# A decoder layer on one core: all engines' calls in a new order, with fewer cleared-tile matmuls

## What is computed

```python
x = x + attn(layernorm(x))            # down-projection, two window branches, feed-forward
x = x + xattn(ctx, layernorm(x))      # causal softmax over 1024 context rows
x = x + ffn(layernorm(x))             # shared expert + 8 routed experts, top 2

def attn(x):
    xi = rmsnorm(x @ down_w + down_b)
    o1 = branch(xi[:, :32], window=10, shift=5)      # 8 heads of 4 channels
    o2 = branch(xi[:, 32:], window=20, shift=10)
    x = x + concat(o1, o2) @ up_w + up_b
    return x + gelu(rmsnorm(x) @ ffn_w1 + ffn_b1) @ ffn_w2 + ffn_b2

def ffn(flat):                                        # 9 experts, 128 -> 256 -> 128
    probs = softmax(flat @ router_w + router_b)
    w = keep_top2(probs)
    h1 = gelu(einsum('td,edh->teh', flat, rw1) + rb1)
    mixed = einsum('ted,te->td', einsum('teh,ehd->ted', h1, rw2) + rb2, w)
    return gelu(flat @ sw1 + sb1) @ sw2 + sb2 + mixed
```

## Time and profile before

| what | value |
|---|---|
| time, three runs | 167.3, 171.09 (median) and 172.68 us |
| profiled execution, its time | 167.33 us |
| profiled execution, its span | 165.5 us |
| PE busy | 150.9 us (91%) |
| VectorE busy | 131.4 us (79%) |
| ScalarE busy | 102.7 us (62%) |
| POOL busy | 42.6 us (26%) |
| mean granted TensorE clock | 0.983 of full speed |
| DMA moved | 13.12 MB |

### The profile page before, as it was taken

How to read it: one execution, slowest core, us unless ns; L and a number is a source line. 1 busy time by engine, 2 the same in 40 slices (tenths; PEclk the granted TensorE clock), 3 DMA queues, 4 the chain that set the end, 5 groups by cost and what they waited for, 6 DMA issues and landing times.

```text
span 165.5 us, 3243 instructions
## 1 busy us (share of the span) xinstructions
PE 150.9 (91%) x1188; PEld 113.4 (68%) x1188; DVE 131.4 (79%) x236; ACT 102.7 (62%) x176; POOL 42.6 (26%) x59
## 2 busy tenths in 40 slices
PE   0798999999989987989899999999999999999980
PEld 0646875659966567788565858768887878887840
DVE  3797898999972999986555659999879866999960
ACT  3113371526173486566787797987987798996830
POOL 5359999202000404005430030033160000000000
PEclk9999999999999999999978999999999999999997
DMA  5999100600870000000096089000000009802002
GB/s 143 365 303 407 61 0 0 117 20 0 143 143 4 0 0 2 0 4 0 0 157 128 8 242 267 5 0 0 0 2 0 4 4 235 272 0 65 0 0 67
DMA packets 6176, 13.12 MB, mean 79 GB/s; under 512 B 672, under 2 KB 2333, under 8 KB 5904
## 3 DMA queue, kind: packets, MB, share of 16 engines
q1 hardware_dynamic: 4902, 9.70, 18.8%
q0 software_dynamic: 944, 2.88, 9.7%
q10 hardware_dynamic: 314, 0.32, 0.7%
HBM read 11.81 MB, written 0.56 MB: 75 GB/s over the span
## 4 chain that ended last, share of the span: by engine, by line
PE 75%; DVE 10%; issue 4%; DMA 2%; POOL 2%; ACT 2%; POOLq 1%; DVEq 0%; ACTq 0%
PE ps L1478 63%; PE ps L1481 5%; PE ps L1754 3%; DMA x_sb<-in_x 2%; PE ps L1548 1%; POOL rstd L582 1%; DVE st L1064 1%; POOL rstd L580 1%; POOLq L94 1%; DVE room L1313 1%; PE ps L1678 1%; DVE room L1058 1%; DVE xf_lo L1261 1%; PE ps L1794 1%; PE ps L1638 1%
## 5 line engine op out<-in xcount | busy, mean ns | idle before, releaser
L1326 DVE TENSOR_TENSOR low<-room,high 128x1024 fp32r<-128x1024 f32 (+1 forms) x20 | 22.1, 1112 | 4.0 <-ACT high L894 3.7
L878 ACT ACTIVATE room<-ps,consts_sb 128x512 f32<-128x512 f32 x36 | 23.2, 682 | 1.5 <-PE ps L1478 0.9
L894 ACT ACTIVATE high<-room 128x1024 fp32r<-128x1024 f32 (+1 forms) x20 | 19.1, 970 | 4.2 <-DVE room L1313 3.5
L580 POOL TENSOR_SCALAR rstd<-mv 128x1 f32<-128x1 f32 (+4 forms) x13 | 5.5, 425 | 54.6 <-DVE mv L1245 32.3
L1478 PE MATMUL ps<-xf_hi,w_hi 128*128 128x512 f32 x36 | 16.7, 463 | 0.0
L1313 DVE TENSOR_TENSOR room<-room,gates 128x1024 f32<-128x1024 f32 (+1 forms) x13 | 14.7, 1136 | 1.0 <-ACT room L878 0.7
L1478 PE MATMUL ps<-xf_lo,w_hi 128*128 128x512 f32 x36 | 14.8, 412 | 0.4 <-DVE xf_lo L1261 0.4
L582 POOL TENSOR_TENSOR rstd<-rstd,minus_half 128x1 f32<-128x1 f32 (+4 forms) x18 | 14.5, 804 | 1.9
L592 POOL TENSOR_SCALAR xn<-x_sb,mv,rstd 128x128 f32<-128x128 f32 x8 | 14.9, 1874 | 0.0
L1478 PE MATMUL ps<-high,w_hi 128*128 128x512 f32 x36 | 14.6, 407 | 0.0
L1478 PE MATMUL ps<-xf_hi,w_lo 128*128 128x512 f32 x36 | 14.6, 405 | 0.0
(11 more groups left out here) (204 smaller groups left out, 342.1 us busy)
## 6 DMA issues: line engine op xcount, KB each, us to landing
gates<-gate_rows SPq DMA_DIRECT2D x12, 256.0 KB, 5.4
moe_w_sb<-in_moe_w SPq DMA_DIRECT2D x2, 1152.0 KB, 11.7
w_lo<-in_moe_w POOLq DMA_DIRECT2D x2, 1152.0 KB, 9.0
ffn_hids<-gate_rows SPq DMA_DIRECT2D x4, 256.0 KB, 3.9
pr<-in_ctx SPq DMA_DIRECT2D x1, 576.0 KB, 6.6
xs<-xn POOLq DMA_DIRECT2D x1, 512.0 KB, 5.2
out<-acc SPq DMA_DIRECT2D x8, 64.0 KB, 1.6
ffn_hids<-in_bias SPq DMA_DIRECT2D x1, 434.7 KB
```

Of the source, the lines that this page charges most:

```text
L580: step(pool.tensor_scalar(dst, src, scale, eps, ALU.mult, ALU.add))
L878: act.activation(hidden_at(q), ps[:, z_bank(q), :], ACT.Gelu, bias=cols_sb[:, i:i + 1]).then_inc(moe_h_ready, 1)
L894: act.activation(split_part(high, h, e, a, z), hidden_part(h, e, a, z), ACT.Copy).then_inc(high_ready, 1)
L1326: dve.tensor_tensor(split_part(low, h, e, a, z), hidden_part(h, e, a, z), split_part(high, h, e, a, z).bitcast(F32), ALU.subtract).then_in ...
```

## The change

The four lists of calls of PE, VectorE, ScalarE and POOL are in a new order. No step is added or removed but for the cleared-tile matmuls: on PE all of them behind the first `qkv_rows` are taken out, and 19 are put in at other places, by a new helper that takes the bank and up to two semaphores. Those ahead of it (nine in all) stay as they were. SP's list is the same.

```diff
@@ PE, the new helper
+            def idle(at, after=None, count=1, also=None, to=1):
+
+                pe.wait_ge(zeros_clear, 1)
+                if after is not None:
+                    pe.wait_ge(after, count)
+                if also is not None:
+                    pe.wait_ge(also, to)
+                mm(ps[:, at, :], zeros16[:, 0:P], zeros16[:])
@@ POOL
             rstd0_pow(0)
-            clear()
             rstd0_pow(1)
             rstd1_pow(0)
             rstd1_pow(1)
+            narrow()
             xn_tiles()
             xs_add()
-            w1_low()
             rstd2_pow(0, 0)
             rstd2_pow(0, 1)
-            narrow()
             rstd3_pow(0, 0)
             rstd3_pow(0, 1)
+            w2_low()
+            w1_low()
+            clear()
             rstd4_pow(0)
             rstd4_pow(1)
             rstd4_pow(2)
             rstd4_pow(3)
-            w2_low()
             rstd2_pow(1, 0)
@@ VectorE, two of many places
             win_margins(1)
+            win_margins(0)
             x_moments(0)
-            win_margins(0)
             x_moments(1)
...
-            x3_tiles(0, 0, 4)
             moe_gate(1, 6)
...
             moe_low(1, 8, 1)
+            x3_tiles(0, 0, 4)
             x3_tiles(1, 0, 1)
```

More of the change, by code:

```diff
@@ L899, in y_copy @@
                 act.activation(x1T[h][:, a * P:z * P], ps[:, 2 + h, a * P:z * P], ACT.Copy).then_inc(y_ready, z - a)
-            half_copy()
             downc_copy()
             bias_split()
+            qkv_copy(1, 0)
+            wqc_copy()
             window_cols(0, 0)
-            qkv_copy(1, 0)
             window_cols(0, 1)
+            half_copy()
             window_cols(1, 1)
+            pu_copy()
             qkv_copy(0, 0)
             w1_high()
-            wqc_copy()
-            pu_copy()
+            w1_negate()
             window_exp(1, 0)
@@ L959, in _ @@
             ffn_gelu(1, 1, 0)
+            wT_copy(0)
             moe_high(0, 0, 0)
+            w_split(0)
+            moe_gelu(0, 1, 1)
             moe_high(0, 0, 1)
-            moe_gelu(0, 1, 1)
-            wT_copy(0)
-            w_split(0)
             moe_gelu(0, 2, 0)
+            moe_gelu(0, 2, 1)
             x1T_copy(1, 0)
-            moe_gelu(0, 2, 1)
             moe_gelu(0, 3, 0)
+            moe_gelu(0, 3, 1)
+            moe_high(0, 1)
             softmax(4)
-            moe_high(0, 1)
+            moe_high(0, 2)
             pT_copy(4)
             softmax(5)
-            moe_gelu(0, 3, 1)
             moe_gelu(0, 4, 0)
+            moe_gelu(0, 4, 1)
             pT_copy(5)
[L976 to L981, removed]
             moe_gelu(0, 5, 0)
             moe_gelu(0, 5, 1)
+            softmax(6)
+            moe_high(0, 3)
+            moe_high(0, 4)
+            pT_copy(6)
+            moe_high(0, 5)
+            softmax(7)
+            moe_gelu(0, 6, 0)
             pT_copy(7)
-            moe_high(0, 4)
-            moe_high(0, 5)
-            moe_gelu(0, 6, 0)
             moe_gelu(0, 6, 1)
-            xf_high(1, 0)
             moe_gelu(0, 7, 0)
@@ L1013, in _ @@
             moe_high(1, 2)
-            gelu_table()
+            moe_high(1, 3)
             moe_gelu(1, 4, 0)
@@ L1348, in _ @@
             xi_norm(1)
-            xs_begin()
             bias_low()
@@ L1364, in _ @@
             window_pairs(1, 1)
+            xs_begin()
             window_product(0, 1)
@@ L1982, in _ @@
             hidden(0, 3, 0)
+            hidden(0, 3, 1)
             scores(4, 0)
             scores(4, 1)
+            hidden(0, 4, 0)
+            scores(5, 0)
+            hidden(0, 4, 1)
             output(0, 0, 0)
-            scores(5, 0)
-            hidden(0, 3, 1)
+            output(0, 0, 1)
             p_columns(4, 0)
             scores(5, 1)
-            hidden(0, 4, 0)
+            output(0, 1, 0)
             p_columns(4, 1)
-            output(0, 0, 1)
+            output(0, 1, 1)
+            scores(6, 0)
             values(4)
             p_columns(5, 0)
-            scores(6, 0)
             scores(6, 1)
+            hidden(0, 5, 0)
             p_columns(5, 1)
-            hidden(0, 4, 1)
-            output(0, 1, 0)
+            hidden(0, 5, 1)
             values(5)
-            hidden(0, 5, 0)
+            output(0, 2, 0)
+            output(0, 2, 1)
             scores(7, 0)
```

246 lines of the change are left out of this document (116 added, 130 removed).

## The result

The changed kernel takes 171.94 us (median of four executions, 170.76 to 172.16) beside 169.63 us of the kernel before: a ratio of 1.024, interval 1.014 to 1.033. The time forecast, 171.5 us, is met; the sum behind it is met in part only. The profiled execution took 170.76 us with a span of 168.9, so 3.4 us more than the one before, where the sum had 2.3. Executions of one kernel differ by up to 9 us, much of it with the clock that they were granted, and every ratio here, with its interval, leaves out those far above their kernel's fastest: two of the four of the kernel before (hence 1.024, where the two medians give 1.014), four of ten of `e1_zeros_back`, four of six of `e12_swap_copy_first`.

What follows compares the result with a forecast made beforehand. PE's own work was taken to set the end from 95.6 us on, so gains lie ahead of the first expert matmul; terms summed to +2.3 us on 167.33, 169.6, plus 1.9 for spread: 171.5 us, range 166.5 to 175.5.

Steps and rivals of the forecast that it cites:

- the sum behind it: Whole kernel: 1.35 - 0.4 + 0 + 0.75 + 0.6 = +2.3 us on the profiled execution's 167.33 us, so 169.6.
- The decisive term: Two weight transfers from POOL: w1_low lands 6.6 us behind w2_low, at 84.55, and hidden(0,0,0) waits for it: +1.35 us.
- Rival B: Weight transfers: both land by 80.8 us and the wait is hidden; 164.2 to 165.9, near 167 with the spread; chance 0.20.
- the gain up to it: Ahead of the transfers: window_scores(1, 1) 2.7 us earlier, of which 1.8 us are left at the end of softmax(1).
- The walk: New order followed call by call with timeline durations: window_scores(1, 1) at 51.0 for 53.73, softmax(1) done at 66.5 for 68.34.
- the first term: Start of hidden(0,0,0), first expert matmul: 84.55 for 83.21 because it waits for w1_low, +1.35 us.
- the missing zeros: Cleared-tile matmuls on PE, 42 down to 28: PE waits instead, priced at 0 unless the clock notices.
- rival C: Window attention: clock falls as zeros are out, value_sum(1, 0) loads take 2.9 us more; 172.5, with spread 174.4; chance 0.25.
- A: The forecast itself: PE waits for w1_low ahead of the expert matmuls; 169.6 us on the profile's clock; chance 0.47.
- Front and copy: Kernel start: win_margins(0) ahead of x_moments(0) gains 0.5 us up to product(1, 0); qkv_copy(0, 0) behind pu_copy costs nothing.
- -0.4, 0 and +0.75: Behind hidden(0,0,0): PE's xf_lo wait goes, -0.4 us; low clock as before, 0; second softmax stage stalls PE, +0.75.
- Tail: Kernel end: half 0's four output issues stand right ahead of the last four in SP's queue, ending 163.3 for 162.65: +0.6 us.

Runs made afterwards that it cites:

- e1_zeros_back: Changed kernel with 12 cleared-tile matmuls put back on PE between 20 and 35 us: median 169.75 us, ratio 1.011 to the kernel before.
- e12_swap_copy_first: Changed kernel with w1_low issued first, four cleared-tile matmuls added and qkv_copy(0,0) back ahead of pu_copy: median 165.9 us, ratio 0.976 to the kernel before.
- e6_after_again: The changed kernel itself, measured again beside the kernel before on one chip: median 170.5 us, ratio 1.017.
- e3_both: Changed kernel with 12 cleared-tile matmuls put back and w1_low issued ahead of w2_low: median 170.55 us beside 169.32 us of the kernel before.
- e10_swap_again: Changed kernel with w1_low issued ahead of w2_low on POOL: median 165.03 us, ratio 0.986 to the kernel before.
- e7: Changed kernel with w1_low issued first and, from hidden(0,0,0) on, the calls in the order of the kernel before: median 166.02 us, ratio 0.989 to the kernel before.

## Why the prediction was right, and where it was not

**The decisive term held.** The two transfers follow each other: the first lands 9.1 us after its issue (9.0 used), the second 5.6 us behind the first (6.6 used). `w1_low` was issued 0.85 us behind `w2_low`, not 1.3. With `w1_low` first, the wait is gone; POOL's wait for `w2_negate`, behind which `w1_low` stood in its queue and which the prediction had in its sum, is as much part of this as the shared engines, and the runs do not separate the two.

The Trainium skill (DMA: Bandwidth & Descriptors, section Issuing engines are not separate DMA queues) says that all DMAs of a core run on the same 16 engines and interleave there. The share of 1.03 over 12.3 us agrees with the first half, for two transfers that are both issued by POOL; of interleaving these two show little, since the first lands as early as one alone.

By the fit of the Trainium skill (the same page, section Anatomy of one DMA), 2.0 us plus bytes over 436 GB/s, both would land about 7.4 us after the first issue, an estimate. The trace has 14.7 us from the first issue to the second landing, and the measurement decides.

Rival B, with both landed by 80.8 us, did not come: the landings are at 81.4 and 87.0.

**The step that failed is the gain up to it.** The walk had `window_scores(1, 1)` at 51.0, 2.7 us early, and `softmax(1)` done at 66.5; it was 55.45 and 70.0. Behind that all went nearly as said: `w2_low` issued 2.3 us after `softmax(1)` (2.45 walked), landings as above. The wait for `w1_low` therefore ended at 87.24 instead of 84.55, and the first term is +4.03 us instead of +1.35.

The difference goes with the clock: the walk took every duration from a trace at full clock, and the sum priced the missing zeros at 0. The score sums came late, so that `window_scores(1, 0)` started 1 us later (28.59 against 27.54 in `e6_after_again`, where the first dip is missing); the four matmuls of the score sides took 1.76 and 2.08 us a pair, against 1.13 and 1.12 in `e3_both`; and the value sums took 7.6 us instead of 5.34. This is what rival C spoke of, and its sign, a low clock between 13 and 70 us, came. C put its 2.9 us on the value sums alone, where the rows have 2.3 there and 2.6 ahead of them; and C came together with A, not in its place.

How much of the 2.7 us the order would give at full clock is not shown, for no run has it there without zeros in the front. With its 12 (`e3_both`) it is 0.7 us. An estimate without them: at the full-clock durations of the score sides the value sums of `e10_swap_again` would start near 37.2 instead of 38.49. Their second part waits for VectorE's last sum, done at 39.35 there, and takes 3.6 us at full clock, so it would end near 43.0, where the walk had 42.5. From there to `window_scores(1, 1)` took 8.2 us in the changed kernel and in `e3_both` alike (8.5 walked), which makes 51.2. By this the order was walked about right, and what the walk lacked was the clock, or the price of the zeros that would hold it.

Between `window_scores(1, 1)` and the end of `softmax(1)` the walk lost 0.9 us to `w2_high` and the copy; the rows show no loss there, 14.55 us against 14.61 before.

**Front and copy.** The L1075 product starts at 8.07 for 8.84: 0.77, where 0.5 was expected (8.16 to 8.47 in the ten later profiles with this front, 8.61 and 8.96 in the two with the old one). `qkv_copy(0, 0)` behind `pu_copy` was priced at nothing; `window_scores(1, 0)` comes 0.3 us late without a dip, so it cost a little.

**Behind hidden(0, 0, 0).** -0.4, 0 and +0.75 make +0.35; measured to the last addition +0.70 (78.98 against 78.28), and +0.03 in `e6_after_again` (78.31). `e7` and `e10` put the order at +0.45. The low clock behind the wait was priced at 0, because the old kernel has such a stretch too, and that was about right: it costs 0.87 us by `e6` against `e10`, and in the old order 78.28 us with it stand against 76.99 without it (`e7`), where 0.37 of the difference are the wait for `xf_lo`. Removing the wait removes this cost as well, which is why the swap gains more than the wait.

**Tail.** +0.6 was wrong. The first four output issues start at 163.01, early enough to be over before the last four: the issues end 2.1 us after the start of the last additions in both kernels. The span closed 1.3 us sooner behind them than before, which no part of the change explains: in the profiled execution of the kernel before one of the eight outputs took 2.9 us from issue to landing, in that of the changed kernel none took more than 1.6.

```profile
163.01 4.32 SPq L555 DMA_DIRECT2D out<-acc  x8
```

So 4.03 + 0.70 - 1.3 = 3.4 us on the profiled executions. A first term that was 2.7 us short met a tail that was 1.9 us too long and 1.9 us added for the spread, of which 1.2 came. That the time is hit more closely than its sum is luck.

## What to carry to other kernels

Where two large transfers are issued from one queue, the one that is read first goes first. Here the second of two landed 14.7 us after the first issue, where one alone takes 9.0; and a transfer also waits for whatever the one ahead of it in the queue waits for, here a copy that held it back by some 5 us. When an order is walked call by call with durations from a trace at full clock, say what each stretch would cost at half the clock, and give that a place in the sum and not only among the rivals. Do not count on a few cleared tiles to prevent a dip: 17 and 12 of them held the clock in some executions and not in others, four did nothing, and at full clock each costs 0.215 us of PE.

## What the hardware showed that was not expected

The granted clock differs between executions of one kernel on one chip: 0.936 to 0.990 over four executions of `e3_both`, with spans of 168.3 to 169.9 and 162.6 us, and 0.945 to 1.000 for the kernel before. The mean clock is not all of it: beside `e6_after_again` the kernel before had a span of 163.9 us at 0.986 and of 168.5 us at 0.987. One such execution says little about a change of this size. In the changed kernel the clock stayed at 1.2 GHz from 84.9 to 91.7 us, 4.5 us into dense work after a wait of 3.1 us. And the last outputs are not of one duration: the span ends 2.85 us after the last issue in the profile of the kernel before, and about 1.6 us after it in all thirteen others, those with the old tail among them; and in `e3_both` the last four issues took 3.12 us instead of 1.77.
